# Chunked scan of a Mamba-2 layer on one core: mask, skip term and scaled x move to other engines, gate in one operation, products in another order

## The chip, the cores and the metric

The program runs on one core of a Trainium2 chip, in one launch. The metric is the time of that launch in microseconds, from runs on the chip. The core has a matrix engine (TensorE, PE in the profile), a vector engine (VectorE, DVE), an activation engine (ScalarE, ACT), a general engine (GpSimd, POOL) and a queue that issues transfers (SyncE, SP). The engines run side by side, each in the order in which its own instructions are written, and meet only at semaphores.

## The reference, cut to what matters

`x` is 2048 rows of 512. The program computes a Mamba-2 mixer and a feed-forward block, then a mixture of experts. The change touches the scan between the mixer's input projection and the feed-forward block:

```python
# per chunk of 128 rows (16 chunks), 16 heads of 64, in 4 groups of heads
dAc    = cumsum(dA)
Lm     = where(tril, exp(dAc[q] - dAc[s]), 0)             # decay, masked
Y_diag = einsum(C, B, Lm, x * dt)
states = einsum(B, exp(dAc[-1] - dAc), x * dt)
carry  = states + exp(dAc[-1]) * carry                    # from chunk to chunk
Y_off  = einsum(C, carry_before, exp(dAc))
y      = Y_diag + Y_off + D * x
y      = rmsnorm(y * silu(z), norm_w) @ out_proj_w
h      = residual + y
h2     = rmsnorm(h, ln2_w)                                # feeds the next stage
```

## The kernel before, in words

`project` (to about 272 us) computes x, B, C, z and dt and stores the rows `cv` (x, B and C of a chunk, channels on partitions) and `zs` (the gate, silu of z) to DRAM. `ssd`, the scan, goes over `TILES` = 16 tiles of 128 rows. `finish` is the feed-forward block and the experts. Data are float32, products of weights are split into three (`hi`/`lo` parts).

The order of each engine's work in `ssd` is written out by hand: one loop over c per engine, in which `e = c - 1` is the tile whose output is being finished and `f = c - 2` the one whose normed rows are turned for the next stage. In a tile PE does:

- `seg` (4 a tile): into one of two banks the mask, by a product of the identity with `mask_r` (L1152), and onto it the row sums of the decay (L1155). ACT's `exps` (L937) makes the decay from it, with the exponential;
- `b_dot_c` (2): B times C (L1164), by which DVE's `score` (L1026) multiplies the decay;
- `cum_rows` (2, L1179): ACT's `cum_exp` (L944) and DVE's `decayed_c` (L1049) make `cexp` of it;
- `diagonal` (2, L1192) and `carried` (2, L1204): 8 products each into the one bank `y_ps`, which DVE's `gate` reads: it adds `dx` (D·x, made by POOL's `skip_x`, L857) and, in a second operation, multiplies by `zs`;
- `states` (L1215), `rows` (L1225: the transposes of the next tile's `cv`, which ACT copies into `xb_row`, L963), `out_proj` (2 of 12 products, L1239), `row_sums` (L1247), `turn_h2` (L1255).

ACT's `high` (L950, L952) makes the upper part and the square of the gated y, DVE's `low` (L1032) the rest. DVE's `outcome` (L1064) makes `hres`; ACT's `h_squares` (L969) sums its squares; POOL's `second_norm` (L900 to L903) norms it, and POOL's `residual` (L894) adds it to x0. POOL also has `decayed_x` (L865), `decay_carry` (L874) and `row_scale` (L884 to L886). DVE's `scaled_x` (L1079) makes `xdt`, x times dt.

SP stores the sum that `residual` made and then loads `cv`, `zs` and `x0` for two tiles later:

```python
eng.wait_ge(s["xh"], e + 1)                      # e = c - 1: POOL's residual(e)
eng.dma_start(dr["xh"][e...], x0[e % 3]).then_inc(xh_st[e % 3], 16)
n = c + 2
ge(eng, xh_st[n % 3], 16 * (n // 3))             # that store has landed
eng.wait_ge(s["gate"], 2 * c + 2)                # and the buffers of tile c are read
load(n)                                          # cv, zs, x0
```

PE's `rows` waits for `cv` and `zs` together (both count on `cv_dma`).

Of the kernel before, what the change touches and what calls it, by code (L numbers as in the profile page):

```python
# [744 lines left out]
def ssd(nc, ins, dr, ident, ones, keep, ffT, first_weights, over):  # L745
# [6 lines left out]
    with ExitStack() as ctx:  # L752
        def sb(name, shape, dt=F32):
# [16 lines left out]
        dx = [sb(f"dx{i}", [P, HPG, P]) for i in range(2)]  # L770
# [18 lines left out]
            "seg", "exp", "cb", "score", "ebc", "ebx", "cexp", "yd", "yo", "ysum", "gate", "hi", "lo", "sq", "sqs", "rs",  # L789
# [57 lines left out]
        def _(eng):  # L847
# [4 lines left out]
            def skip_x(c, a):  # L852

                if a == 0:
                    eng.wait_ge(cv_dma[c % 2], 32 * (c // 2 + 1))
                ge(eng, s["ysum"], 2 * (c - 1) + a + 1)
                eng.tensor_tensor(dx[a][:, :, :], cv[c % 2][:, a, :].unsqueeze(1).broadcast_to([P, HPG, P]),  # L857
                                  d_col[:, a * HPG:(a + 1) * HPG].unsqueeze(2).broadcast_to([P, HPG, P]), ALU.mult)\
                   .then_inc(s["dx"], 1)
# [51 lines left out]
            eng.wait_ge(s["v_dma"], 16 * 9)  # L911
            for c in range(TILES + 1):
                e = c - 1
                if c < TILES:
                    for a in range(2):
                        skip_x(c, a)
                    if c + 1 < TILES:
                        decayed_x(c)
                        decay_carry(c)
                if e >= 0:  # L920
                    row_scale(e)
                    if c < TILES:
                        residual(e)
                    second_norm(e)
                    if c == TILES:
                        residual(e)

        @block.scalar
        def _(eng):
            def exps(c, hg):  # L930
# [8 lines left out]
                last.then_inc(s["exp"], 1)  # L939

# [37 lines left out]

            rows(0)
            for c in range(TILES + 2):  # L980
                e, f = c - 1, c - 2
                now, late, later = c < TILES, 0 <= e < TILES, 0 <= f
                if now:
                    exps(c, 0)
                    cum_exp(c, 0)
                    exps(c, 1)
# [4 lines left out]
                if now:  # L991
                    exps(c, 2)
                if c == 0:
                    out_high(HPG, NB)
# [4 lines left out]
                if now:  # L999
                    exps(c, 3)  # L1000
                    cum_exp(c, 1)
                    high(c, 0)
                    if c + 1 < TILES:
                        rows(c + 1)
                if late and now:
                    h_squares(e)

        @block.vector
        def _(eng):
            def gate(c, a):  # L1010

                eng.wait_ge(s["yo"], 2 * c + a + 1)
                eng.wait_ge(s["dx"], 2 * c + a + 1)
                ge(eng, s["lo"], 2 * (c - 1) + a + 1)
                ge(eng, s["sq"], 2 * (c - 1) + a + 1)
                if a == 0:
                    eng.wait_ge(cv_dma[c % 2], 32 * (c // 2 + 1))
                eng.tensor_tensor(yg[a][:, :, :], y_ps[:, :].rearrange("p (j q) -> p j q", j=HPG), dx[a][:, :, :], ALU.add)\
                   .then_inc(s["ysum"], 1)
                eng.wait_ge(s["ysum"], 2 * c + a + 1)  # L1020
                eng.tensor_tensor(yg[a][:, :, :], yg[a][:, :, :], zs[c % 2][:, a, :, :], ALU.mult).then_inc(s["gate"], 1)
# [52 lines left out]
            def scaled_x(c):  # L1074
                g, u = group(c)
                eng.wait_ge(s["xb_row"], c + 1)
                ge(eng, s["yd"], 2 * (c - 1))
                ge(eng, s["xdd"], c - 1)
                eng.tensor_tensor(xdt[c % 2][:, :].rearrange("p (g r d) -> p g r d", g=NG, r=HPG),  # L1079
                                  xb_row[c % 2][:, 0, :].rearrange("p (g d) -> p g d", g=NG).unsqueeze(2)  # L1080
                                  .broadcast_to([P, NG, HPG, HD]),
                                  dt_all[:, g, u * HEADS:(u + 1) * HEADS].rearrange("p (g r) -> p g r", g=NG).unsqueeze(3)
                                  .broadcast_to([P, NG, HPG, HD]), ALU.mult).then_inc(s["xdt"], 1)

# [20 lines left out]
            scaled_x(0)  # L1105
            for c in range(TILES + 2):
                e, f = c - 1, c - 2
                now, late, later = c < TILES, 0 <= e < TILES, 0 <= f
                if late:
                    gate(e, 1)  # L1110
                if now:
                    score(c, 0)
                    decayed_c(c, 0)
                    score(c, 1)
                if c == 0:
                    out_low(0, HPG)
                if late:
                    low(e, 1)
                    if now:
                        new_carry(e)  # L1120
                    squares(e)
                if now:
                    gate(c, 0)
                if late:
                    row_sums(e)
                if later and c != TILES:
                    h2_low(f)
                if now:
                    score(c, 2)
                    score(c, 3)  # L1130
                    if c == 0:
                        out_low(HPG, NB)
                    decayed_c(c, 1)
                    low(c, 0)
# [5 lines left out]
                if now:  # L1140
                    if c + 1 < TILES:
                        scaled_x(c + 1)
# [3 lines left out]
        def _(eng):  # L1146
            def seg(c, hg):

                g, u = group(c)
                ge(eng, s["exp"], 4 * c + hg - 1)  # L1150
                ps = seg_ps[hg % 2]
                eng.matmul(ps[:, :], ident_r[:, :], mask_r[:, :].unsqueeze(1).broadcast_to([P, HPG, P]),  # L1152
                           start=True, stop=False)
                m = u * NG + hg
                eng.matmul(ps[:, :], sel[:, m:m + 1].broadcast_to([P, P]), bd[:, g, :, :].rearrange("p j q -> p (j q)"),  # L1155
                           start=False, stop=True).then_inc(s["seg"], 1)
# [25 lines left out]
            def diagonal(c, a):  # L1182

                ge(eng, s["ysum"], 2 * c + a)
# [3 lines left out]
                for j in range(HPG):  # L1188
                    for b in range(2):
# [3 lines left out]
                                          decay[hg][:, j, :], start=(j == 0), stop=False, skip_group_check=True)  # L1193
# [64 lines left out]
            rows(0)  # L1258
            for c in range(TILES + 2):
# [963 lines left out]
```

## Time and profile before

| | |
|---|---|
| time, median of 3 runs (lowest to highest) | 1429.9 us (1429.3 to 1430.69) |
| the profiled execution's own time | 1429.85 us |
| its span in the profile | 1427.8 us |
| busy over the span: PE, DVE, ACT, POOL | 96%, 67%, 45%, 32% |
| the scan: first and last instruction of PE | 272.99 us to 563.5 us |
| from a tile's first `seg` to the next tile's | 17.33 us |

The span is what the profiler recorded of one execution; 2.05 us of its time lie around it. In a timeline a row is an instruction, or several in a row of one kind ("x4"), with its start and its length; the next one on the same engine can start before the length is over, because an engine overlaps the end of one with the start of the next, so what an instruction costs its engine in a busy stretch is the distance of two starts. In brackets stands how long the engine had been idle and what released it.

### The profile page before, as it was taken

The numbers are of one execution on the slowest core, as the hardware profiler recorded it, in microseconds if no ns is written. First come the engines' busy times: TensorE is split into PE (matmuls) and PEld (weight loads), VectorE is DVE, ScalarE is ACT, GpSimd is POOL, SyncE is SP. The second block draws the span as 40 slices with busy tenths as digits, with TensorE's granted clock in tenths as the row PEclk, the third lists the DMA queues.
The fourth block names the chain that finished last, engine by engine and source line by source line (L and its number), as shares of the span: only waits on it lengthen the run. The fifth ranks groups of instructions, "written<-read, shape, count | busy, mean of one in ns | idle before, by whom it ended". The sixth has DMA issues, their size and how long they took to land.

```text
span 1427.8 us, 20607 instructions
## 1 busy us (share of the span) xinstructions
PE 1374.9 (96%) x7240; PEld 1103.4 (77%) x7240; DVE 953.5 (67%) x1327; ACT 640.9 (45%) x1123; POOL 460.4 (32%) x447
## 2 busy tenths in 40 slices
PE   6899999899999997999999999999999889999998
PEld 5677778666666665888888888888887689999997
DVE  7789788789999996233333333333346879999997
ACT  5445445545555554221111212111212358888886
POOL 2112121357777775111010101110101026566563
PEclk9999999999999998999999999999999979999999
DMA  6133123722222232400000000002034924444331
GB/s 208 60 118 118 60 89 140 221 97 104 104 104 104 104 111 81 156 30 15 30 29 15 29 15 29 15 30 96 0 111 155 334 81 74 77 71 75 72 49 22
DMA packets 69047, 122.62 MB, mean 86 GB/s; under 512 B 11743, under 2 KB 28127, under 8 KB 68960
## 3 DMA queue, kind: packets, MB, share of 16 engines
q1 hardware_dynamic: 59696, 103.67, 21.3%
q0 software_dynamic: 8736, 16.79, 6.8%
q8 instruction: 49, 0.80, 0.2%
q10 hardware_dynamic: 528, 1.05, 0.2%
q14 instruction: 38, 0.31, 0.1%
HBM read 81.37 MB, written 43.78 MB: 88 GB/s over the span
## 4 chain that ended last, share of the span: by engine, by line
PE 57%; DVE 2%; ACT 0%; issue 0%; DMA 0%; POOL 0%; DVEq 0%; ACTq 0%; POOLq 0%
PE fin_bank L1934 54%; PE fin_bank L2075 1%; PE fin_bank L2094 1%; DVE onehot L1843 0%; PE fin_bank L2002 0%; DMA xs<-xn_rows,idx 0%; PE fin_bank L1990 0%; DVE ff_w_lo L1735 0%; ACT gu_hi L1626 0%; DVE fi_bn L1770 0%; ACT ff_w_hi L1604 0%; DVE gu_lo L1864 0%; PE fin_bank L2067 0%; POOL out_dram L1558 0%; PE fin_bank L2000 0%
## 5 line engine op out<-in xcount | busy, mean ns | idle before, releaser
L1697 DVE TENSOR_TENSOR ff_prod<-ff_prod,fin_bank 128x512 f32<-128x512 f32 x64 | 44.0, 688 | 263.0 <-PE fin_bank L1934 263.0
L1934 PE MATMUL fin_bank<-ff_hT_hi,ff_w_hi 128*128 128x512 f32 x512 | 202.8, 396 | 3.2 <-DVE ff_w_lo L1705 3.2
L1934 PE MATMUL fin_bank<-ff_hT_lo,ff_w_hi 128*128 128x512 f32 x512 | 202.7, 396 | 0.0
L1934 PE MATMUL fin_bank<-ff_hT_hi,ff_w_lo 128*128 128x512 f32 x512 | 202.6, 396 | 0.0
L1488 POOL TENSOR_TENSOR ff_w_lo<-ff_stage,ff_w_hi 128x1024 fp32r<-128x1024 f32 (+1 forms) x24 | 56.5, 2355 | 410.9 <-ACT ff_w_hi L1594 406.0
L1579 ACT ACTIVATE ff_prod<-fin_bank 128x512 f32<-128x512 f32 x64 | 38.3, 598 | 230.8 <-PE fin_bank L1934 230.7
L687 PE MATMUL pj_bank<-hT_hi,w_in_hi 128*128 128x512 f32 x324 | 131.5, 406 | 6.1 <-DVE w_in_lo L587 5.0
L555 DVE SCALAR_TENSOR_TENSOR conv_acc<-raw,conv_w,conv_acc 128x512 f32<-128x512 f32 x144 | 108.1, 751 | 37.2 <-ACT raw L355 32.1
L687 PE MATMUL pj_bank<-hT_lo,w_in_hi 128*128 128x512 f32 x324 | 128.6, 397 | 0.0
L687 PE MATMUL pj_bank<-hT_hi,w_in_lo 128*128 128x512 f32 x324 | 128.1, 395 | 0.0
L1864 DVE TENSOR_TENSOR gu_lo<-wx,gu_hi 128x1408 fp32r<-128x1408 f32 (+1 forms) x79 | 125.0, 1621 | 1.9 <-ACT gu_hi L1626 1.8
L1582 ACT ACTIVATE ff_p_hi<-ff_prod 128x512 fp32r<-128x512 f32 x64 | 40.5, 632 | 190.3 <-DVE ff_prod L1697 190.3
L1626 ACT ACTIVATE gu_hi<-wx 128x1408 fp32r (+1 forms) x79 | 109.8, 1391 | 19.4 <-DMA wx<-in_L_ffn_Wd_dram 15.6
L937 ACT ACTIVATE decay<-ss_bank,keep_neg_cum 128x128 f32<-128x128 f32 x256 | 73.0, 368 | 100.4 <-PE ss_bank L1155 100.4
L1934 PEld LDWEIGHTS fin_bank<-ff_hT_hi,ff_w_hi 128*128 128x128 f32 x512 | 96.4, 188 | 27.1 <-issue 3.6
L1755 DVE TENSOR_TENSOR acc_rows<-fin_bank,acc_rows 128x512 f32<-128x512 f32 x128 | 87.5, 689 | 40.7 <-PE fin_bank L1934 40.3
L1934 PEld LDWEIGHTS fin_bank<-ff_hT_hi,ff_w_lo 128*128 128x128 f32 x512 | 96.3, 188 | 23.7
L1934 PEld LDWEIGHTS fin_bank<-ff_hT_lo,ff_w_hi 128*128 128x128 f32 x512 | 96.3, 188 | 23.5
L1934 PE MATMUL fin_bank<-gu_hi,xe_hi 128*128 128x352 f32 x312 | 105.1, 337 | 0.0
L1934 PE MATMUL fin_bank<-gu_lo,xe_hi 128*128 128x352 f32 x312 | 101.0, 324 | 0.0
L1934 PE MATMUL fin_bank<-gu_hi,xe_lo 128*128 128x352 f32 x312 | 100.8, 323 | 0.0
L1934 PE MATMUL fin_bank<-ff_w_lo,ff_p_hi 128*128 128x512 f32 x256 | 100.1, 391 | 0.0
(299 smaller groups left out, 3171.4 us busy)
## 6 DMA issues: line engine op xcount, KB each, us to landing
cv_rows<-cst SPq DMA_DIRECT2D x12, 1024.0 KB, 4.2
cv<-cv_rows SPq DMA_DIRECT2D x16, 768.0 KB, 4.3
zs_rows<-zst SPq DMA_DIRECT2D x8, 1024.0 KB, 6.5
zs<-zs_rows SPq DMA_DIRECT2D x16, 512.0 KB, 5.3
wx<-in_L_ffn_Wg_dram SPq DMA_DIRECT2D x8, 704.0 KB, 8.9
wx<-in_L_ffn_Wu_dram SPq DMA_DIRECT2D x8, 704.0 KB, 9.4
x<-_attn_hidden_states_dram SPq DMA_DIRECT2D x16, 256.0 KB, 5.5
xh_rows<-x SPq DMA_DIRECT2D x16, 256.0 KB, 2.0
```

The lines of the kernel that those rows point to most:

```text
L555: eng.scalar_tensor_tensor(acc[m % 4][:, :], raw[m % 3][:, t:t + GR], conv_w[:, ch, t:t + 1], acc[m % 4][:, :], ALU.mult, ALU.add).then_in ...
L687: mm = eng.matmul(ps[:, :], (w_hi, w_lo)[a][:, k, col:col + P], x[b][:, k, :], start=(k == 0 and t == 0), stop=(k == KD - 1 and t == 2))
L937: last = eng.activation(decay[hg][:, j, :], seg_ps[hg % 2][:, j * P:(j + 1) * P], ACT.Exp, bias=neg_cum[:, g, h:h + 1])
L1488: eng.tensor_tensor(w_lo[par][j][:, cols], stage[j][:, cols], w_hi[par][j][:, cols].bitcast(F32), ALU.subtract).then_inc(s["w_lo"], 1)
L1579: eng.activation(prod[c][:, :], gate_ps[c][:, :], ACT.Silu).then_inc(s["silu"], 1)
L1582: eng.activation(p_hi[k % 2][:, c, :], prod[c][:, :], ACT.Copy).then_inc(s["p_hi"], 1)
L1626: eng.activation(out, raw_part(own[j], kind), ACT.Copy).then_inc(s["ew_hi"], 1)
L1697: eng.tensor_tensor(prod[c][:, :], prod[c][:, :], up_ps[c][:, :], ALU.mult).then_inc(s["prod"], 1)
L1755: eng.tensor_tensor(row, down_ps[t][:, :], row, ALU.add).then_inc(s["add"], 1)
L1864: eng.tensor_tensor(lo, raw_part(own[j], kind), hi.bitcast(F32), ALU.subtract).then_inc(s["ew_lo"], 1)
L1934: mm = eng.matmul(ps, w[a], x[b], start=first and i == 0, stop=last and i == 2)
L2075: last = eng.transpose(xT_ps[:, k * P:(k + 1) * P], xs[j % UN][:, k * P:(k + 1) * P], ident[:, :])
```

## The change

- PE's `seg` no longer writes the mask, but for the first two: ACT's new `mask` copies `mask_r` into the bank as soon as `exps` has read it, and PE's one product adds to it.
- `skip_x` moves from POOL to ACT. It writes D·x into `y_ps` (four operations of 128 columns), `diagonal` adds to it, and `gate` is one operation, `y_ps` times `zs`. `y_ps` is written again only after `gate` has read it.
- `scaled_x` moves from DVE to POOL, behind `row_scale`, and `residual` from ahead of `second_norm` to behind it.
- PE's products stand in another order, and `seg(c + 1, 0)` comes at the end of tile c. ACT's and DVE's order is changed too.

```diff
@@ POOL
-            def skip_x(c, a):
-                ...
-                ge(eng, s["ysum"], 2 * (c - 1) + a + 1)
-                eng.tensor_tensor(dx[a][:, :, :], cv[c % 2][:, a, :].unsqueeze(1)..., d_col[...]..., ALU.mult)
+            def scaled_x(c):
+                eng.wait_ge(s["xb_row"], c + 1)
+                ge(eng, s["yd"], 2 * (c - 1))
+                ge(eng, s["xdd"], c - 1)
+                eng.tensor_tensor(xdt[c % 2]..., xb_row[c % 2]..., dt_all..., ALU.mult).then_inc(s["xdt"], 1)
...
+            scaled_x(0)
             for c in range(TILES + 1):
                 e = c - 1
-                if c < TILES:
-                    for a in range(2):
-                        skip_x(c, a)
-                    if c + 1 < TILES:
-                        decayed_x(c)
-                        decay_carry(c)
+                if c + 1 < TILES:
+                    decayed_x(c)
+                    decay_carry(c)
                 if e >= 0:
                     row_scale(e)
-                    if c < TILES:
-                        residual(e)
+                if c + 1 < TILES:
+                    scaled_x(c + 1)
+                if e >= 0:
                     second_norm(e)
-                    if c == TILES:
-                        residual(e)
+                    residual(e)
@@ ACT
+            def mask(c, hg):
+                n = 4 * c + hg
+                if n < 4 * TILES - 2:
+                    eng.wait_ge(s["exp"], n + 1)
+                    eng.activation(seg_ps[hg % 2]..., mask_r..., ACT.Copy).then_inc(s["masked"], 1)
...
+            def skip_x(c, a):
+                ...
+                ge(eng, s["gate"], 2 * c + a)
+                for j in range(HPG):
+                    last = eng.activation(y_ps[:, j * P:(j + 1) * P], cv[c % 2][:, a, :], ACT.Copy,
+                                          scale=d_col[:, a * HPG + j:a * HPG + j + 1])
+                last.then_inc(s["dx"], 1)
@@ DVE
             def gate(c, a):
                 eng.wait_ge(s["yo"], 2 * c + a + 1)
-                eng.wait_ge(s["dx"], 2 * c + a + 1)
...
-                eng.tensor_tensor(yg[a]..., y_ps..., dx[a]..., ALU.add).then_inc(s["ysum"], 1)
-                eng.wait_ge(s["ysum"], 2 * c + a + 1)
-                eng.tensor_tensor(yg[a]..., yg[a]..., zs[c % 2]..., ALU.mult).then_inc(s["gate"], 1)
+                eng.tensor_tensor(yg[a]..., y_ps..., zs[c % 2]..., ALU.mult).then_inc(s["gate"], 1)
@@ PE
             def seg(c, hg):
-                ge(eng, s["exp"], 4 * c + hg - 1)
-                eng.matmul(ps[:, :], ident_r[:, :], mask_r..., start=True, stop=False)
+                ps, n = seg_ps[hg % 2], 4 * c + hg
+                if n < 2:
+                    eng.matmul(ps[:, :], ident_r[:, :], mask_r..., start=True, stop=False)
+                else:
+                    eng.wait_ge(s["masked"], n - 1)
...
             def diagonal(c, a):
-                ge(eng, s["ysum"], 2 * c + a)
+                eng.wait_ge(s["dx"], 2 * c + a + 1)
```

The order of the instructions on two engines follows; line numbers of the changed kernel are its own. First PE, in one tile in the middle, of the kernel before: from the transposes of the next tile (L1225) to the first product of `out_proj` (L1239).

```order
L1225 MATMUL ss_bank<-ident,cv 128x128 x4
L1192 MATMUL ss_bank<-decay,xdt 64x128 x8
L1204 MATMUL ss_bank<-cexp,carry 64x128 x8
L1215 MATMUL ss_bank<-xdd,xb_row 64x256 x4
L1152 MATMUL ss_bank<-keep_mask_r,keep_ident_r 128x512
L1155 MATMUL ss_bank<-keep_bd,keep_sel 128x512
L1179 MATMUL ss_bank<-keep_bd,sel_wide 128x512
L1164 MATMUL ss_bank<-cv 128x512 x2
L1152 MATMUL ss_bank<-keep_mask_r,keep_ident_r 128x512
L1155 MATMUL ss_bank<-keep_bd,keep_sel 128x512
L1239 MATMUL ss_bank<-wo_hi,y_hi 128x512
```

And PE of the changed kernel, of the same place, from the two products ahead of the transposes (now L1239; `out_proj` is L1253, `seg` L1169, `cum_rows` L1193, `b_dot_c` L1178).

```order
L1193 MATMUL ss_bank<-keep_bd,sel_wide 128x512
L1169 MATMUL ss_bank<-keep_bd,keep_sel 128x512
L1239 MATMUL ss_bank<-ident,cv 128x128 x4
L1206 MATMUL ss_bank<-decay,xdt 64x128 x8
L1218 MATMUL ss_bank<-cexp,carry 64x128 x8
L1229 MATMUL ss_bank<-xdd,xb_row 64x256 x4
L1178 MATMUL ss_bank<-cv 128x512 x2
L1193 MATMUL ss_bank<-keep_bd,sel_wide 128x512
L1169 MATMUL ss_bank<-keep_bd,keep_sel 128x512
L1253 MATMUL ss_bank<-wo_hi,y_hi 128x512
```

The mask's products are gone, and the products that use the whole array stand together: `cum_rows` is next to `seg`, and the first `seg` of the next tile has moved ahead of the transposes.

POOL, one tile, of the kernel before: `row_scale` (L884 to L886), `residual` (L894), `second_norm` (L900 to L903), `skip_x`, `decayed_x`, `decay_carry`.

```order
L884 TENSOR_SCALAR small<-small 128x1
L885 TENSOR_TENSOR small<-small,ss_half_neg 128x1
L886 TENSOR_SCALAR small<-small 128x1
L894 TENSOR_TENSOR x_1<-hres,x_1 128x512
L900 TENSOR_SCALAR small<-small 128x1
L901 TENSOR_TENSOR small<-small,ss_half_neg 128x1
L902 TENSOR_SCALAR h_1<-hres,small 128x512
L903 TENSOR_TENSOR h_1<-h_1,ln_row 128x512
L857 TENSOR_TENSOR dx<-cv,keep_d_col 128x512 x2
L865 TENSOR_TENSOR xdd<-xdt,keep_exp_suf 128x1024
L874 TENSOR_TENSOR carry<-carry,keep_chunk_decay 128x512
```

And POOL of the changed kernel, the same tile (`scaled_x` is L856, `second_norm` L901 to L904, `residual` L895).

```order
L885 TENSOR_SCALAR small<-small 128x1
L886 TENSOR_TENSOR small<-small,ss_half_neg 128x1
L887 TENSOR_SCALAR small<-small 128x1
L856 TENSOR_TENSOR xdt<-xb_row,keep_dt 128x1024
L901 TENSOR_SCALAR small<-small 128x1
L902 TENSOR_TENSOR small<-small,ss_half_neg 128x1
L903 TENSOR_SCALAR h_1<-hres,small 128x512
L904 TENSOR_TENSOR h_1<-h_1,ln_row 128x512
L895 TENSOR_TENSOR x_1<-hres,x_1 128x512
L866 TENSOR_TENSOR xdd<-xdt,keep_exp_suf 128x1024
L875 TENSOR_TENSOR carry<-carry,keep_chunk_decay 128x512
```

`residual` now stands behind the transposes' consumer `scaled_x` and behind the whole of `second_norm`. ACT, one tile of the changed kernel, from the second `cum_exp` (L952) to the next tile's first `skip_x` (L995); `mask` is L945, `exps` L936, `h_squares` L977, `high` L958 and L960.

```order
L952 ACTIVATE ebx<-ss_bank 128x512
L971 ACTIVATE xb_row<-ss_bank 128x512
L936 ACTIVATE decay<-ss_bank,keep_neg_cum 128x128 x4
L945 ACTIVATE ss_bank<-keep_mask_r 128x512
L977 ACTIVATE ss_junk,small<-hres 128x512
L952 ACTIVATE ebx<-ss_bank 128x512
L936 ACTIVATE decay<-ss_bank,keep_neg_cum 128x128 x4
L958 ACTIVATE y_hi<-yg 128x512
L960 ACTIVATE sq<-yg 128x512
L995 ACTIVATE ss_bank<-cv,keep_d_col 128x128 x4
```

Here `exps` of the next tile's first group and `mask` have come between the copy of the transposed rows (L971) and `h_squares` (L977), and `skip_x` stands behind `exps` and `high`.

## Rows read from the trace of the kernel before

**Rows 1.** Windows, one stretch: busy us (and instructions) of each engine, PEclk, DMA

```profile
400.00:450.00 50.00, 49.76 (x366) 33.92 (x366) 46.30 (x56) 26.62 (x74) 36.24 (x36) 1.00 0.30 110
```

**Rows 2.** Timeline, PE, one tile: start, length, what, count [idle before <-releaser]

```profile
396.61 0.50 PE L1152 MATMUL ss_bank<-keep_mask_r,keep_ident_r 128*128 128x512 f32 x1
396.95 0.40 PE L1155 MATMUL ss_bank<-keep_bd,keep_sel 128*128 128x512 f32 x1
397.18 0.39 PE L1179 MATMUL ss_bank<-keep_bd,sel_wide 128*128 128x512 f32 x1
...
399.13 0.39 PE L1239 MATMUL ss_bank<-wo_hi,y_hi 128*128 128x512 f32 x1
...
402.02 1.09 PE L1192 MATMUL ss_bank<-decay,xdt 128*64 128x128 f32 x16
...
410.35 0.60 PE L1225 MATMUL ss_bank<-ident,cv 128*128 128x128 f32 x4
...
413.94 0.50 PE L1152 MATMUL ss_bank<-keep_mask_r,keep_ident_r 128*128 128x512 f32 x1
```

**Rows 3.** Timeline, ACT, the later half of the same tile

```profile
407.52 1.14 ACT L937 ACTIVATE decay<-ss_bank,keep_neg_cum 128x128 f32<-128x128 f32 x4 [1.13 <-PE ss_bank L1155]
408.53 0.61 ACT L944 ACTIVATE ebx<-ss_bank 128x512 f32<-128x512 f32 x1
409.01 0.66 ACT L950 ACTIVATE y_hi<-yg 128x512 fp32r<-128x512 f32 x1
409.53 0.66 ACT L952 ACTIVATE sq<-yg 128x512 f32<-128x512 f32 x1
410.98 0.60 ACT L963 ACTIVATE xb_row<-ss_bank 128x512 f32<-128x512 f32 x1 [0.80 <-PE ss_bank L1225]
411.48 0.62 ACT L969 ACTIVATE ss_junk<-hres 128x512 bf16<-128x512 f32 x1
412.00 0.19 ACT L969 ACTIVATION_READ_ACCUMULATOR ss_junk<-hres 128x1 f32 x1
```

**Rows 4.** Timeline, POOL, the next tile

```profile
411.38 1.26 POOL L894 TENSOR_TENSOR x<-hres,x 128x512 f32<-128x512 f32 x1 [3.39 <-DVE hres L1064]
412.73 1.05 POOL L900 TENSOR_SCALAR small<-small 128x1 f32<-128x1 f32 x1
...
414.72 1.58 POOL L902 TENSOR_SCALAR h<-hres,small 128x512 f32<-128x512 f32 x1
416.39 1.29 POOL L903 TENSOR_TENSOR h<-h,ln_row 128x512 f32<-128x512 f32 x1
417.63 2.93 POOL L857 TENSOR_TENSOR dx<-cv,keep_d_col 128x512 f32<-128x512 f32 x2
420.53 1.90 POOL L865 TENSOR_TENSOR xdd<-xdt,keep_exp_suf 128x1024 f32<-128x1024 f32 x1
```

**Rows 5.** Timeline, POOL, after the last tile

```profile
551.24 0.25 POOL L900 TENSOR_SCALAR small<-small 128x1 f32<-128x1 f32 x1
```

**Rows 6.** Timeline, DVE, beside rows 4

```profile
411.61 2.12 DVE L1079 TENSOR_TENSOR xdt<-xb_row,keep_dt 128x1024 f32<-128x1024 f32 x1 [0.31 <-ACT xb_row L963]
...
416.66 1.56 DVE L1049 TENSOR_TENSOR cexp<-cv,ebx 128x512 f32<-128x512 f32 x1
```

**Rows 7.** Timeline, SP's queue: start and length of each issue

```profile
412.68 0.32 SPq L825 DMA_DIRECT2D xh_rows<-x  x1
416.01 0.32 SPq L812 DMA_DIRECT2D cv<-cv_rows  x1
```

**Rows 8.** DMA issues of 300 to 545 us: count, KB each, us to landing

```profile
zs<-zs_rows SPq DMA_DIRECT2D x13, 512.0 KB, 5.3
xh_rows<-x SPq DMA_DIRECT2D x14, 256.0 KB, 2.0
```

**Rows 9.** Timeline, ACT, the first tile

```profile
277.38 2.57 ACT L976 ACTIVATE wo_hi<-wo_raw,keep_normw 128x512 fp32r<-128x512 f32 x4
```

**Rows 10.** Timeline, PE, the first tile

```profile
278.37 1.09 PE L1192 MATMUL ss_bank<-decay,xdt 128*64 128x128 f32 x16 [2.04 <-DVE decay L1026]
```

More of the change, by code:

```diff
@@ L977, in out_high @@
                        .then_inc(s["wo_hi"], 1)
+            def skip_x(c, a):
+                if a == 0:
+                    eng.wait_ge(cv_dma[c % 2], 32 * (c // 2 + 1))
+                if c + a == 0:
+                    eng.wait_ge(s["seg"], 1)
+                ge(eng, s["gate"], 2 * c + a)
[3 more added lines that the diff above has]
+                last.then_inc(s["dx"], 1)
             rows(0)
+            eng.wait_ge(s["v_dma"], 16 * 9)
+            exps(0, 0)
+            mask(0, 0)
             for c in range(TILES + 2):
@@ L991, in _ @@
                 if now:
+                    skip_x(c, 0)
+                    mask(c, 1)
                     exps(c, 2)
+                    mask(c, 2)
                 if c == 0:
@@ L1000, in _ @@
                     exps(c, 3)
+                    high(c, 0)
+                    skip_x(c, 1)
+                    mask(c, 3)
                     cum_exp(c, 1)
-                    high(c, 0)
                     if c + 1 < TILES:
                         rows(c + 1)
+                        exps(c + 1, 0)
+                        mask(c + 1, 0)
                 if late and now:
@@ L1072, in last_norm @@
                    .then_inc(s["h2_step"], 2)
[L1074 to L1083, printed above, removed]
             def new_carry(c):
@@ L1110, in _ @@
                     gate(e, 1)
+                    if now:
+                        new_carry(e)
                 if now:
+                    decayed_c(c, 0)
                     score(c, 0)
-                    decayed_c(c, 0)
                     score(c, 1)
@@ L1258, in _ @@
             rows(0)
+            eng.matmul(y_ps[:, :], ident_r[:, :], mask_r[:, :].unsqueeze(1).broadcast_to([P, HPG, P]), start=True, stop=True)
+            seg(0, 0)
             for c in range(TILES + 2):
@@ L1269, in _ @@
                 if now:
+                    seg(c, 2)
                     diagonal(c, 0)
-                    seg(c, 2)
                     carried(c, 0)
-                if late and now:
-                    row_sums(e)
                 if later and c != TILES:
@@ L1278, in _ @@
                     b_dot_c(c, 1)
+                if late and now:
+                    row_sums(e)
+                if now:
                     seg(c, 3)
-                    cum_rows(c, 1)
                 if late:
                     out_proj(e, 1, None if now else row_sums)
+                if now:
+                    cum_rows(c, 1)
+                    if c + 1 < TILES:
+                        seg(c + 1, 0)
                 if c == TILES:
```

46 lines of the change are left out of this document (20 added, 26 removed).

## The prediction, made before the changed kernel ran

> **What bounds the kernel now.** I began with the windows. In the middle of the scan PE is busy for 49.76 of 50 us at the full granted clock, DVE for 46.30, POOL for 36.24, ACT for 26.62 [rows 1]. Then the timeline of PE over one tile: from one tile's first `seg` to the next tile's lie 17.33 us (396.61 to 413.94), and no row between them carries a wait [rows 2]. So in the tiles of the middle PE is the bound. ACT waits often, but only for PE (1.13 us before `exps`, 0.80 us before the copy into `xb_row`) [rows 3]. POOL's row for `residual` shows 3.39 us of idle time [rows 4]. SP issues the store of `residual`'s sum at 412.68 and `cv` at 416.01 [rows 7]; that `cv` serves transposes that PE makes at about 427.7, one period of 17.33 behind those at 410.35 [rows 2]. With `zs` issued some 0.35 later and landing in 5.3 us [rows 8], the data are there at about 421.7: 6 us to spare. That reserve is what I follow below, because the change spends it.
>
> **What PE saves.** A mask product holds PE for 0.34 us (396.61 to 396.95), the one behind it for 0.23 (396.95 to 397.18) [rows 2]. I read the extra 0.11 as the price of going from products on part of the array to whole ones: it comes with the first whole product, not with the mask. On the way back there is about 0.1 as well: 12 products of `out_proj` take 2.89 us up to the `diagonal` behind them (399.13 to 402.02), 0.13 more than 12 times 0.23 [rows 2]. Removed per tile: 4 x 0.23 = 0.92. The new order goes from part to whole three times a tile and not five: 2 x (0.11 + 0.1) = 0.4. Together 1.3, so PE's own work falls from 17.33 to 16.0 us a tile.
>
> **What the others gain and lose.** ACT now has 26.62 / 50 x 17.33 = 9.2 us a tile. It gets four `mask` of 128x512 and eight operations of 128x128 for D·x. No row shows ACT writing a bank; the nearest are copies of 128x512 at a distance of 0.50 to 0.52 us and 0.60 to 0.66 long, and four of 128x128 at 1.01 us together and 1.14 long [rows 3]. I bound a `mask` between 0.45 and 0.65 and take 0.50; `skip_x` between 0.8 and 1.15, taking 1.0. ACT comes to 9.2 + 4 x 0.50 + 2 x 1.0 = 13.2 us, not a bound by load. The Trainium skill, "PSUM — Partial Sum Buffer", specifications, says that ScalarE's write is faster into PSUM than into SBUF; no row here shows it, and by it both would stand at the lower end, 0.05 us a `mask` less. DVE loses `scaled_x` (2.12 us [rows 6]) and two additions and is no bound. POOL loses two `dx` (2.93 us) and gets `scaled_x`: as many elements as `decayed_x` in 1.90 us or as both `dx` in 2.93 [rows 4]. I take 1.9 to 2.3, near `decayed_x`, which also reads one full tensor and one spread along 64.
>
> **New waits of PE.** `y_ps` must hold D·x before `diagonal`. For the first half ACT can start only when the product of `cum_rows` is through, about 0.5 us after its start: then `cum_exp` 0.49 (408.53 to 409.01), `exps` 1.01, `high` 2 x 0.52, `skip_x` 1.14 with its length [rows 3], and the handovers, 0.5 + 0.49 + 1.01 + 1.04 + 1.14 + 0.1 = 4.3 us. PE itself needs 0.34 + 0.23 + 2.89 + 0.23 = 3.7 from there to `diagonal`. That is a stall of 0.55 a tile (0.3 to 0.8). For the second half ACT has, from `seg(c, 3)` on, `exps`, `high`, `skip_x`, `mask`, `cum_exp`, and then DVE `decayed_c`: 0.4 + 1.01 + 1.04 + 1.0 + 0.5 + 0.62 + 0.7 + 0.1 = 5.4 us, against 0.24 + 2.8 + 0.5 + 0.6 + 1.0 = 5.2 on PE to `carried`: 0.2 more (0 to 0.6). Behind the waiting `skip_x` on ACT stand `mask` and the next `exps`, which PE needs only later. PE with its stalls: 16.0 + 0.55 + 0.2 = 16.7 us.
>
> **The loop that spends the reserve.** SP loads tile c + 2 only when the store of `residual(c - 1)` has landed. Before, `residual` ran as soon as `hres` was there. Now it stands behind `scaled_x(c + 1)`, which waits for the transposes `rows(c + 1)`, and behind `second_norm`. And `rows(c + 2)`, one tile on, waits for that load. This closes a loop of one tile:
>
> - landing of `zs` to the transposes and their copy's start on ACT: 0.05 + 0.63 (410.35 to 410.98) [rows 2, 3] = 0.68;
> - ACT: copy 0.50, `exps` with its full length 1.14 (`mask` waits for it), `mask` 0.50, `h_squares` 0.52 + 0.19 [rows 3], handovers 0.15: 3.0. POOL's `scaled_x` lies beside it: 0.60 + 1.9 = 2.5;
> - `second_norm`: 4.95 from 412.73 to 417.68, less 0.80, because its first step took 1.05 there while DVE ran `xdt`, and 0.25 alone [rows 4, 5, 6]: 4.15;
> - `residual` 1.26 [rows 4] and 0.05: 1.31;
> - the store 2.0 [rows 8] and two handovers: 2.1;
> - `cv` issued, `zs` 0.35 later and 5.3 to its landing [rows 7, 8]: 5.65, with handover 5.7.
>
> The sum is 16.9 us. Without handovers and with a `mask` of 0.45 it is 16.5. To it comes what POOL loses to DVE: DVE's `cexp` of the next tile falls, by this count, into `second_norm`'s two long steps. Rows 4 and 6 show such meetings: the first step stretched from 0.25 to 1.05 beside `xdt`, `cexp` to 1.56 beside L903. I add 0.2 and take 17.1. That is above PE's 16.7, so PE would wait for DMA at the transposes, some 0.4 us a tile, and nearly all of the 1.3 us is given back.
>
> **The sum.** The loop counts between `rows(2)` and `rows(15)`, 13 periods: 13 x (17.1 - 17.33) = -3.0 us. At the edges: in the first tile four copies of `out_proj`'s weights, 2.57 us [rows 9], stand ahead of the first `skip_x` on ACT, so the first `diagonal` (278.37, where PE had already waited 2.04 us [rows 10]) comes some 2.8 us later. I estimate that 1.6 of it are left when tile 1 starts, and that tile 1, which PE still bounds, gives 0.9 back: +0.7. The last tile has no transposes behind it and saves 1.3 less the stalls: -0.6; the one-operation `gate` in the tail, -0.3. Edges -0.2, all -3.2. From the profiled execution's own 1429.85 (span 1427.8 and 2.05 around it), 0.05 under the median of 1429.9, that is 1426.7 us. The stages behind the scan don't change.
>
> **The rivals.**
>
> PE stays the bound. If `mask`, the norm or the landing are some tenths shorter, the loop is under 16.7 and PE's stalls decide: 13 x (16.7 - 17.33) - 0.2 = -8.4, 1421.5 us. With no stall either, 16.0: -17.5, 1412.4. For it speaks that the loop's lower bound is 16.5 and that PE is now busy without a gap; against it that this needs six terms at their short end, and ACT two chains as well.
>
> The loop is longer than before's period, slower. The place is POOL, from `scaled_x` to the end of `residual`; the price is one lost turn against DVE for each meeting. If `cexp` gets in ahead of the norm's last step, and DVE's `low` of the other half ahead of `residual`, each costs up to DVE's 0.6 to 0.7: 16.9 + 0.6 + 0.6 = 18.1, or 17.7 with one whole and a third of the other. It decides from 17.35 on. At 17.7: 13 x 0.37 - 0.2 = +4.6, 1434.4 us; at 18.1: +9.8, 1439.6. `scaled_x` at 2.93 instead of 1.9 would make POOL later than ACT by 0.5 and adds as much. For it speaks that in rows 4 and 6 nearly every operation of POOL meets one of DVE's; against it that `xdt`, DVE's longest operation with two tensors in SBUF, is gone from DVE. The Trainium skill, "SBUF — State Buffer", on engine ports, has the shared port pair of VectorE and GpSimd as an exclusive lock for a whole instruction, so that the later one blocks fully. By that rule the first step's 1.05 is waiting, and rows 4 and 6 agree (`xdt` ends at 413.73, the step at 413.78). By it a `cexp` that gets in costs `second_norm` about 0.65 each tile, the loop is 17.6 and the time about 1433.
>
> The change doesn't do what it says. `skip_x` could be so late that `diagonal` waits for it 1.3 us and more: then PE alone has 17.3 and nothing is won, 1430. It would need ACT operations of twice the rows' length.
>
> **How the numbers follow.** Loop between 16.9 and 17.55: 0.5, time 1424 to 1432.5; below 17.12, which half of this case is, the gain is over 0.2%. PE bound: 0.25, all faster. Loop over 17.55: 0.22, all slower. No effect by late `skip_x`: 0.03. About 0.2%, 2.9 us, is what a measurement of this kernel can tell from no change. Faster 0.25 + 0.25 = 0.50, within 0.28, slower 0.22. The range leaves out the stall-free end at 1412.4 and the meetings that all go against POOL: 1414 to 1438. The likeliest case's own range is 1424 to 1432.5.
>
> **What would show it.** Right: in the changed kernel's PE timeline a wait of some tenths to 1 us before each set of transposes, released by the DMA into `zs` or `cv`; `cv` issued some 2 us after the store, and the store issued a third of a tile into the next tile, not at its end; a period of 17 us; a wait of about 0.5 us before the first `diagonal` of each tile; mask products gone, `mask` near 0.5. Wrong: transposes without a wait and a period under 16.8 (the loop is shorter than I count), a period of 17.5 and more with `second_norm` over 4.7 (the meetings), or PE idle before `seg` (a `mask` that comes too late). A scan that is no different but a time that is would mean that I looked at the wrong stage.

## The result, and the profile after

| | before | changed |
|---|---|---|
| time, median (lowest to highest) of 6 runs each | 1429.38 us (1428.86 to 1430.69) | 1437.28 us (1434.46 to 1438.6) |
| span of the profiled execution | 1427.8 us | 1435.9 us |
| busy over the span: PE, DVE, ACT, POOL | 96%, 67%, 45%, 32% | 95%, 62%, 49%, 31% |

The changed kernel takes 1.0049 times as long (95% interval 1.0039 to 1.0059). Slightly faster was forecast, 1426.7 us. The measured time lies just inside the stated range (1414 to 1438), but at its slow end, which only the second rival reached, and the direction is the wrong one. The window in the middle of the scan [rows 1], of the changed kernel, with the same columns:

```profile
400.00:450.00 50.00, 46.51 (x334) 31.46 (x330) 33.83 (x46) 39.58 (x109) 32.89 (x33) 1.00 0.31 111
```

PE now has gaps, 3.5 us of 50, at the full clock. The waits of the scan's middle (300 to 548 us) of the changed kernel, us in total, times, longest, tell for whom:

```profile
POOL xdt L856 <- ACT xb_row L971: 58.8, 14, 6.3
PE ss_bank L1206 <- ACT ss_bank L995: 8.9, 14, 0.6
PE ss_bank L1239 <- DMA zs<-zs_rows: 8.4, 12, 2.4
```

The waits of the kernel before show none of PE for DMA there; now it waits 12 times at the transposes (L1239), for `zs`, and 14 times, 0.6 us each, for ACT's `skip_x` (L995) at the first `diagonal` of a tile. The second stall that was forecast, before `carried`, shows only twice here.

One turn of the loop, row by row. PE's timeline of the changed kernel [rows 2]:

```profile
414.80 0.65 PE L1239 MATMUL ss_bank<-ident,cv 128*128 128x128 f32 x4 [0.43 <-DMA zs<-zs_rows]
...
423.90 1.09 PE L1206 MATMUL ss_bank<-decay,xdt 128*64 128x128 f32 x16 [0.64 <-ACT ss_bank L995]
...
432.26 0.66 PE L1239 MATMUL ss_bank<-ident,cv 128*128 128x128 f32 x4 [0.70 <-DMA zs<-zs_rows]
```

ACT's [rows 3]:

```profile
413.20 1.26 ACT L995 ACTIVATE ss_bank<-cv,keep_d_col 128x128 f32<-128x128 f32 x4
414.38 0.60 ACT L945 ACTIVATE ss_bank<-keep_mask_r 128x512 f32<-128x512 f32 x1
414.89 0.60 ACT L952 ACTIVATE ebx<-ss_bank 128x512 f32<-128x512 f32 x1
415.49 0.60 ACT L971 ACTIVATE xb_row<-ss_bank 128x512 f32<-128x512 f32 x1
415.99 1.14 ACT L936 ACTIVATE decay<-ss_bank,keep_neg_cum 128x128 f32<-128x128 f32 x4
417.16 0.60 ACT L945 ACTIVATE ss_bank<-keep_mask_r 128x512 f32<-128x512 f32 x1
417.69 0.61 ACT L977 ACTIVATE ss_junk<-hres 128x512 bf16<-128x512 f32 x1
```

POOL's [rows 4]:

```profile
416.17 1.90 POOL L856 TENSOR_TENSOR xdt<-xb_row,keep_dt 128x1024 f32<-128x1024 f32 x1 [3.95 <-ACT xb_row L971]
418.49 0.19 POOL L901 TENSOR_SCALAR small<-small 128x1 f32<-128x1 f32 x1 [0.41 <-ACT ss_junk L977]
...
421.09 1.45 POOL L904 TENSOR_TENSOR h<-h,ln_row 128x512 f32<-128x512 f32 x1
422.51 1.79 POOL L895 TENSOR_TENSOR x<-hres,x 128x512 f32<-128x512 f32 x1
```

DVE's, beside it [rows 6]:

```profile
422.48 0.69 DVE L1058 TENSOR_TENSOR y_lo<-yg,y_hi 128x512 fp32r<-128x512 f32 x1
```

And SP's queue [rows 7]:

```profile
424.33 0.32 SPq L824 DMA_DIRECT2D xh_rows<-x  x1
426.46 0.32 SPq L811 DMA_DIRECT2D cv<-cv_rows  x1
426.82 0.43 SPq L812 DMA_DIRECT2D zs<-zs_rows  x1
```

Each step starts where the one before it ends, read from these rows: transposes 414.80, copy 415.49, norm 418.49, `residual` 422.51, store 424.33, `cv` 426.46, next transposes 432.26. The period is 17.46 us where it was 17.33.

Where the 8.1 us of the two spans come from, by the starts of the transposes (`rows(n)`), with `finish` from its first product:

| stretch | before | changed | difference | forecast |
|---|---|---|---|---|
| `rows(0)`, the scan's start | 272.99 | 274.04 | +1.05 | 0 |
| `rows(0)` to `rows(2)` | 33.44 | 36.43 | +3.0 | +0.7 |
| `rows(2)` to `rows(15)`, 13 periods | 225.11 | 228.6 | +3.5 | -3.0 |
| `rows(15)` to `finish` | 35.21 | 35.16 | -0.05 | -0.9 |
| the rest of the program | | | +0.6 | 0 |

The first and the last line are outside the change. In the traces of all the kernels here `rows(0)` lies between 272.34 and 274.06 us, with the same code ahead of it, so +1.05 is the spread of single executions; +0.6 is of the same size.

Eleven of the 13 periods have a mean of 17.38. The other two are 19.19 and 18.24, each with a late landing in it. In the first it is a store's. The DMA issues of the changed kernel from 510 to 518 us: count, KB, us to landing [rows 8]:

```profile
xh_rows<-x SPq DMA_DIRECT2D x1, 256.0 KB, 3.9
```

In SP's queue `cv` stands behind it:

```profile
511.17 0.32 SPq L824 DMA_DIRECT2D xh_rows<-x  x1
515.07 0.32 SPq L811 DMA_DIRECT2D cv<-cv_rows  x1
```

The other stores of the scan landed in 2.0 to 2.2 us. PE waited 2.42 us, and in the next window its granted clock was 0.83, a mean of the two levels (1.2 and 2.4 GHz), where 400 to 450 us had 1.00. In the second period the `zs` issued at 532.87 landed in 6.2 us, 0.9 more than the usual 5.3. The window:

```profile
520.00:530.00 10.00, 9.17 (x60) 6.52 (x61) 4.58 (x8) 5.24 (x15) 6.78 (x6) 0.83 0.07 26
```

### The profile page after: what moved, and what is told of

The parts are those of the page before. It is cut to its first block, busy times and chain, and to the rows that moved or that the text cites. A ratio compares the mean times of both kernels' runs of the same rounds, so it can differ in the third digit from the quotient of the medians.

```text
span 1435.9 us, 20597 instructions
## 1 busy us (share of the span) xinstructions
PE 1361.5 (95%) x7179; PEld 1095.8 (76%) x7179; DVE 889.7 (62%) x1279; ACT 710.3 (49%) x1313; POOL 438.3 (31%) x431
## 3 DMA queue, kind: packets, MB, share of 16 engines
q10 hardware_dynamic: 528, 1.05, 0.2%
## 4 chain that ended last, share of the span: by engine, by line
PE 56%; DVE 2%; issue 1%; DMA 0%; ACT 0%; POOL 0%; DVEq 0%; POOLq 0%; ACTq 0%
PE fin_bank L1953 53%; PE fin_bank L2094 1%; PE fin_bank L2113 1%; DVE onehot L1862 0%; DMA xs<-xn_rows,idx 0%; PE fin_bank L2021 0%; PE fin_bank L2009 0%; DVE ff_w_lo L1754 0%; DMA out_dram<-result_rows,idx 0%; DVE fi_bn L1789 0%; ACT ff_w_hi L1623 0%; PE fin_bank L2086 0%; POOL out_dram L1577 0%; DVE oj L1857 0%; PE fin_bank L2019 0%
## 5 line engine op out<-in xcount | busy, mean ns | idle before, releaser
L1953 PE MATMUL fin_bank<-ff_w_hi,ff_p_hi 128*128 128x512 f32 x256 | 99.9, 390 | 0.0
```

The costliest lines, as they stand in the source:

```text
L1953: mm = eng.matmul(ps, w[a], x[b], start=first and i == 0, stop=last and i == 2)
```

## Experiments

Every ratio is to the kernel before, on the same chip, with its 95% interval. Three chips were used, on which the kernel before took 1429.66 (the runs a), 1430.36 (b1, b2, b4, c1) and 1429.89 us (b3, d1); where two runs of different groups differ by less than that, nothing is read from it. The theory: the loop through POOL, the store and the load of `cv` and `zs` sets the period. The rivals: PE's stalls behind ACT, or DVE.

**Open the loop, two ways.** a1_residual_ahead:

```diff
                 if e >= 0:
-                    second_norm(e)
                     residual(e)
+                    second_norm(e)
```

> The changed kernel with one edit: POOL does residual(e) ahead of second_norm(e), still behind scaled_x. Theory (a loop of one tile: transposes, scaled_x, second_norm, residual, store, load, transposes): the store goes out some 4 us earlier, the waits for DMA before the transposes are gone, the tile is PE's own 16.7 to 16.8 us (17.46 less the wait of 0.70), 13 x (16.76 - 17.58) = -10.7 us against the changed kernel, about 1427. Rival (the DMA wait only covers another one: h2 comes late for turn_h2, or ACT's chains stretch to the same length): 1433 or more.

a2_load_before_store, SP:

```diff
+                    load_rows(n)                 # cv, zs: waits only for tile c's readers
                 if e >= 0:
                     eng.wait_ge(s["xh"], e + 1)
                     eng.dma_start(dr["xh"]..., x0[e % 3]...)
-                    load(n)                      # cv, zs, x0
+                    load_x(n)                    # x0 alone
```

> The changed kernel with one edit in SP's order: cv and zs of tile c + 2 are loaded when tile c's buffers are read, ahead of the wait for residual(c - 1) and its store; only x0 is loaded behind the store. POOL's order stays. Theory of the loop: cut at its other end, same effect, about 1427, with cv issued at the start of a tile. Rival (the transfers themselves are slower beside the new order of work, or residual is late for another reader): no change from the changed kernel, 1437.

1430.71 us, ratio 1.0004 (0.9995 to 1.0013), and 1431.09 us, 1.0008 (0.9999 to 1.0017). In both PE has no wait for DMA, and the period is 17.12 to 17.17 in each tile. One edit is on POOL, the other on SP, and what they share is that the load no longer waits for the norm: the loop is the cause of the wait for DMA. Both times are 4 us over the expected 1427, because a stall that the changed kernel hardly shows has come out (below). In POOL's and SP's timelines of a1_residual_ahead the store is now at 417.60:

```profile
416.13 1.45 POOL L895 TENSOR_TENSOR x<-hres,x 128x512 f32<-128x512 f32 x1
```

```profile
417.60 0.32 SPq L824 DMA_DIRECT2D xh_rows<-x  x1
419.62 0.32 SPq L811 DMA_DIRECT2D cv<-cv_rows  x1
```

With the loop open a late landing costs nothing: the `zs` issued at 488.59 landed in 7.1 us, and the periods around it stayed at 17.15 and 17.14. What is left of PE's idle in a tile stands in its timeline:

```profile
414.55 1.09 PE L1218 MATMUL ss_bank<-cexp,carry 64*64 64x128 f32 x16 [0.53 <-DVE cexp L1075]
422.03 1.09 PE L1206 MATMUL ss_bank<-decay,xdt 128*64 128x128 f32 x16 [0.63 <-ACT ss_bank L995]
```

Counted from start to start, less what the product ahead takes, that is 0.60 and 0.68; PE's own work is 17.15 - 1.28 = 15.87.

**Lengthen the loop.** a3_longer_loop: POOL makes one more product of `decay_carry`'s shape (1.04 us), which nobody reads, between `second_norm` and `residual`.

```diff
                     second_norm(e)
+                    extra_work(e)
                     residual(e)
```

> The changed kernel with one operation more on POOL between second_norm and residual, of the shape of decay_carry (1.04 us), whose result nobody reads. POOL is idle some 5 us a tile. Theory of the loop: every period gets about 1.0 to 1.1 us longer, 13 x 1.05 = +14, about 1451. Rival (POOL has idle time, the wait for DMA is a matter of transfer time): no change, 1437.

1446.3 us, ratio 1.0115 (1.0099 to 1.013): 9.0 over the changed kernel. `rows(2)` to `rows(15)` take 237.09, 0.65 a period more than in the changed kernel (228.6) for 1.04 put in; expected were 1451 us and 1.05. PE's waits are where the theory has them:

```profile
PE ss_bank L1246 <- DMA zs<-zs_rows: 18.7, 13, 1.8
```

Without the changed kernel's two late landings the mean of its other eleven periods is 17.38, and this kernel's mean is 18.24: 0.86 more. Its rows tell where the rest is. First POOL, then DVE and SP:

```profile
410.04 1.57 POOL L882 TENSOR_TENSOR extra<-ln_row,keep_chunk_decay 128x512 f32<-128x512 f32 x1
411.58 1.27 POOL L901 TENSOR_TENSOR x<-hres,x 128x512 f32<-128x512 f32 x1
```

```profile
410.03 0.69 DVE L1065 TENSOR_TENSOR y_lo<-yg,y_hi 128x512 fp32r<-128x512 f32 x1
```

```profile
412.88 0.32 SPq L825 DMA_DIRECT2D xh_rows<-x  x1
```

The new operation takes 1.57 us beside `y_lo`, and `residual`, now behind it, is back at 1.27 where the changed kernel has 1.79. So the store goes out 10.57 us behind the transposes in the mean of the 13 tiles, where the eleven tiles of the changed kernel have 9.59: 0.98 of the 1.04 has come through. Then `zs` happened to land in 5.21 us here and in 5.34 there, 0.13 less. That is the 0.86.

**The stalls alone, and both.** b1_skip_early: each `skip_x` goes ahead of what it stood behind on ACT, of `cum_exp`, `exps` and `high` in the first half of the tile and of `exps` and `high` in the second. b2_both: b1 with `residual` ahead of the norm.

```diff
+                    skip_x(c, 0)
                     cum_exp(c, 0)
                     exps(c, 1)
                 ...
                     high(e, 1)
-                    skip_x(c, 0)
                     mask(c, 1)
...
+                    skip_x(c, 1)
                     exps(c, 3)
                     high(c, 0)
-                    skip_x(c, 1)
                     mask(c, 3)
```

> The changed kernel with one edit in ACT's order: skip_x(c, 0) ahead of cum_exp(c, 0), skip_x(c, 1) ahead of exps(c, 3), where ACT sits idle for 1.7 and 1.1 us. POOL's order stays, so the loop over residual, store and load stays. Theory (the loop sets the period, PE's stalls for D*x lie in its shadow): the waits before diagonal and carried (0.68 and up to 0.6 us) go, the wait for DMA before the transposes grows by as much, the time stays within 2 us of the changed kernel's 1437. Rival (PE's own stalls set the period and the DMA wait follows them): 13 x 1.2 = -16, 1421.

> Both edits: residual ahead of second_norm on POOL, and skip_x where ACT is idle. With residual ahead alone the tile was 17.15 us, of which 0.68 before the first diagonal and 0.60 before the second carried were waits, so PE's own work is 15.87. Theory: both waits go, 13 x (15.9 - 17.15) = -16 and some 1 to 2 us in the first and last tile, about 1413. Rival (the next limit is close, DVE's lock with POOL or ACT's queue): 1418 to 1424.

b1: 1436.18 us, 1.0037 (1.0023 to 1.0051). The wait at `diagonal` is gone, and the time is that of the changed kernel within the two intervals; the idle has moved to the transposes (8.4 us in the changed kernel):

```profile
PE ss_bank L1239 <- DMA zs<-zs_rows: 17.5, 12, 2.2
```

b2: 1413.49 us, 0.9883 (0.9868 to 0.9898), as expected, period 15.84 to 15.85. Its window:

```profile
400.00:450.00 50.00, 50.00 (x384) 34.71 (x380) 39.59 (x51) 43.27 (x118) 36.06 (x35) 1.00 0.35 129
```

With the loop open, the stalls are worth 17.2 us (1430.71 to 1413.49); with it closed, about 1, which these runs cannot tell from nothing. The two waits hide each other.

**The first tile.** b3_first_tile (the changed kernel) and b4_all (b2) put ACT's copies of `out_proj`'s weights behind the masks of the first tile, and DVE's part of the last four at that tile's end. The cut shows the first four; the last four go behind `mask(1, 0)`:

```diff
-                if c == 0:
-                    out_high(0, HPG)
                 ...
                     mask(c, 1)
+                if c == 0:
+                    out_high(0, HPG)
```

> The changed kernel with one edit, in the first tile alone: ACT's copies of out_proj's weights stand behind the masks instead of ahead of the first skip_x, and DVE's share of them at the end of that tile. Theory (the first tile's late skip_x is a cost of its own, separate from the loop): the first diagonal comes about 2.5 us earlier, rows(2) 1 to 2 us earlier, the 13 periods behind it as in the changed kernel (about 228 us): 1 to 2 us less than the changed kernel, 1435.5. Rival (the loop absorbs it: the store and the load set rows(2) too, so what the first tile gains is waited for at rows(2) or rows(3)): rows(3) at the same time as in the changed kernel, time the same within 0.5 us.

> As the one with both edits, and in the first tile ACT makes the copies of out_proj's weights later: the first four behind mask(0, 1), the last four behind mask(1, 0), DVE's lower parts of the last four at the tile's end. Theory: the first tile's diagonals no longer wait for 2.5 us of copies, PE's clock does not fall there, another -2 to -4 us, about 1410. Rival (the copies are only waited for later, by out_proj of tile 0): no gain, 1413.

b3: 1434.78 us, 1.0029 (1.002 to 1.0038), 2.5 under the changed kernel, where 1 to 2 were expected. From `rows(0)` to `rows(3)` it takes 51.53, where the changed kernel takes 53.94: the first tile is a cost of its own. (2.5 is about the spread of the changed kernel's own runs; the trace, not the median, carries this.) b4: 1412.33 us, 0.9876 (0.9861 to 0.9891), the fastest of all; 1.2 gained where 2 to 4 were expected. `rows(0)` to `rows(2)` falls from 38.07 in b2 to 36.33 only, and a new wait for `score` has come up. DVE's second four copies now run from 292.17 for 4.39 us, with `gate` behind them at 296.48; that they cause the wait is likely, but the steps between were not followed. Its PE, first tiles:

```profile
301.07 1.98 PE L1207 MATMUL ss_bank<-decay,xdt 128*64 128x128 f32 x16 [4.01 <-DVE decay L1053]
```

**Parts alone, on the kernel before.** a4_mask_alone gives only the mask to ACT:

```diff
-                eng.matmul(ps..., ident_r..., mask_r..., start=True, stop=False)
+                if n < 2:
+                    eng.matmul(ps..., ident_r..., mask_r..., start=True, stop=False)
+                else:
+                    eng.wait_ge(s["wide"], n)    # ACT's mask
```

> The kernel before with only the mask moved: ACT copies the mask into the banks (62 copies of 0.52 us), PE keeps one product for each seg; order, skip term, gate and scaled_x as before. Theory 1 (0.23 us of a mask product are its own, 0.11 are the switch to whole products): 62 x 0.23 = -14.3, about 1415. Theory 2 (all 0.34 are the mask's): -21, about 1408. Rival (DVE, 46.3 of 50 us busy, becomes the bound at 16.1 to 16.5 us a tile with its waits): -8 to -12, 1418 to 1421.

1426.05 us, 0.9973 (0.9962 to 0.9984), period 17.06: a smaller gain than either theory or the rival expected (1408 to 1421). PE's timeline of it:

```profile
397.60 0.50 PE L1172 MATMUL ss_bank<-keep_bd,keep_sel 128*128 128x512 f32 x1
397.93 0.39 PE L1256 MATMUL ss_bank<-wo_hi,y_hi 128*128 128x512 f32 x1
398.16 0.39 PE L1256 MATMUL ss_bank<-wo_lo,y_hi 128*128 128x512 f32 x1
...
404.12 0.38 PE L1264 MATMUL ss_bank<-ones,sqs 128*128 128x2 f32 x2 [0.66 <-DVE sqs L1054]
```

The `seg` product now has the distance 0.33 that the mask's had [rows 2], and the ones behind it 0.23. PE's own work is 17.06 - 0.67 = 16.39, 0.94 less: four times 0.23. What PE does not get is the 0.67, a wait for DVE at `row_sums`, where DVE's timeline has no wait between 395.60 and 407.19.

c1_mask_scaled: that kernel with `scaled_x` on POOL, behind `residual` and ahead of the norm.

> The kernel before with the mask moved to ACT and scaled_x moved to POOL, behind residual and ahead of second_norm; skip term, two-operation gate and PE's order as before. With the mask alone the tile was 17.06 us, of which PE waited 0.67 for DVE's sum of squares. Theory (DVE is the bound there, and 2.12 us of it are scaled_x): PE's own 16.4 a tile, 14 x -0.67 = -9, about 1417. Rival (POOL, with both dx and scaled_x 14.5 us and its locks against DVE, becomes late): 1424 or more.

1426.71 us, 0.9975 (0.9965 to 0.9986), where 1417 was expected: no gain over a4 in all. The middle gains a little, the period is 16.94 (1.7 us over the 13); the first tiles lose it again, `rows(0)` to `rows(2)` takes 36.34 where a4 has 33.41. There PE waits for a `cexp` that stands behind DVE's copies of the weights:

```profile
293.49 1.97 PE L1222 MATMUL ss_bank<-cexp,carry 64*64 64x128 f32 x16 [4.68 <-DVE cexp L1079]
```

PE's wait at `row_sums` stayed as it was although DVE's busy time in the window fell from 47.32 to 44.70:

```profile
PE ss_bank L1265 <- DVE sqs L1069: 8.9, 14, 0.7
```

So DVE's load does not set it. Neither expectation had this. In c1's trace the square that `sqs` sums is ready at 403.44, and `sqs` starts at 404.83: ahead of it on DVE stand `score`, which waits 0.40 us for an `exps` of ACT, then `y_lo` and the new carry. That this chain is the cause was not tried.

d1_before_residual_behind: only `residual` moves, behind the norm.

```diff
                     row_scale(e)
+                    second_norm(e)
                     if c < TILES:
                         residual(e)
-                    second_norm(e)
```

> The kernel before, with POOL's residual moved behind second_norm and nothing else. Theory (a loop, closed only because scaled_x stands on POOL ahead of the norm): here the norm starts with hres, at the place where residual was, so residual ends about 5 us later and the store lies at about 417.7 instead of 412.7. cv was issued 1.3 us behind the store's landing before, for another wait, so its issue moves by some 3.8 us only, to about 419.8, and zs lands at about 425.5, 2 us ahead of the transposes (427.7). No wait of PE at the transposes, period 17.33, time within 0.1% of before. Rival (residual's place alone is what costs): a wait of PE for DMA at the transposes in each tile and a period of 17.5 and more, +3 us and more.

1433.42 us, 1.0022 (1.0013 to 1.0031): I expected nothing, and it costs 3.5 us. Counted from the transposes, the store goes out after 8.19 us and not after 2.33 [rows 2, 7]: 5.9 later and not 5. The norm now waits for ACT's `h_squares`, which `residual` used to cover, 0.9, and `residual` itself takes 1.78. POOL's timeline:

```profile
412.54 0.62 POOL L900 TENSOR_SCALAR small<-small 128x1 f32<-128x1 f32 x1 [3.86 <-ACT ss_junk L969]
...
417.00 1.78 POOL L894 TENSOR_TENSOR x<-hres,x 128x512 f32<-128x512 f32 x1
```

In most tiles the 1.5 us left suffice (period 17.34). Two stores landed late, in 3.9 and 4.3 us, and SP's queue shows what the second does:

```profile
365.56 0.32 SPq L825 DMA_DIRECT2D xh_rows<-x  x1
369.90 0.32 SPq L812 DMA_DIRECT2D cv<-cv_rows  x1
```

4.34 us from store to `cv`. The transposes waited, and the two periods were 17.70 and 18.23; the next, 17.74, has a wait of 0.42 for DVE's `sqs` and a `zs` that landed in 7.4 us. In the profiled execution `rows(2)` to `rows(15)` is 1.9 us longer than before. It was the fastest of the eleven; that the others had more of it I did not see.

This displaced tile also shows what stretches `residual`. Here it starts 0.30 ahead of DVE's `cexp`, and `cexp` is the long one:

```profile
381.97 1.30 POOL L894 TENSOR_TENSOR x<-hres,x 128x512 f32<-128x512 f32 x1
```

```profile
382.27 1.54 DVE L1049 TENSOR_TENSOR cexp<-cv,ebx 128x512 f32<-128x512 f32 x1
```

In the tile shown above `cexp` starts 0.07 ahead of `residual` (417.00), and `residual` is the long one, 1.78:

```profile
416.93 0.68 DVE L1049 TENSOR_TENSOR cexp<-cv,ebx 128x512 f32<-128x512 f32 x1
```

In the same kernel, the one that comes second is stretched.

## Why the prediction was wrong

The loop was right; three sizes were too small, and together they turned a small gain into a loss. The time came out on the far side of the point that the second rival named: "It decides from 17.35 on". Of the forecast's -3.2 us, 3.6 were lost to the longer loop, 2.7 to two late landings, 2.3 in the first tile and 0.9 in the last; that makes +6.3, and the rest of the 8.1 is the first and the last line of the table. A loop of 17.38 alone would have given no change (13 x 0.05 - 0.2), not a loss.

- **The loop: 17.1 forecast, 17.46 in the tile shown, 17.38 in the mean of the undisturbed ones.** Term by term, forecast and measured: transposes to copy 0.68, 0.69; copy to norm 3.0, 3.00; `second_norm` 4.15, 4.02; `residual` 1.31, 1.82; store 2.1, 2.13; load 5.7, 5.80. The step that failed is the term for `residual` and its meeting with DVE. I had put the meetings at 0.2 in all, and on `cexp` in the norm. The meeting came from `y_lo`, with `residual` itself, in twelve tiles, in which it takes 1.79 to 1.82 us: `y_lo` ran from 422.48 to 423.17 and `residual` took 1.79 instead of 1.26 [rows 4], 0.53 more for the 0.66 that `y_lo` still ran. The sum `sqs` does not do it: in a3 `residual` runs beside it and takes 1.27. The Trainium skill, "SBUF — State Buffer", on engine ports, says of a VectorE instruction with two inputs in SBUF, as `y_lo` has, and a GpSimd instruction that reads SBUF that the one that starts later is blocked until the other is over. These rows agree, with 0.53 for 0.66. I had it as the cause of a rival, with 0.65 and on the norm, and should have laid DVE's new order beside POOL's to see which operation falls there. The norm was 0.13 shorter than forecast, so the mean is 17.38 and not more: 13 x (17.38 - 17.1) = 3.6 us.
- **The late landings.** "the store 2.0" and 5.3 for `zs` were medians. In this chain each landing counts: a store of 3.9 us cost 19.19 - 17.38 = 1.8, and a `zs` of 6.2 us most of 18.24 - 17.38 = 0.9. The kernel before had a `zs` of 6.4 us (issued at 381.73) and lost nothing by it. That the changed kernel's six runs spread over 4 us and the before's over 2 fits this, but only one execution was profiled.
- **The first tile: +0.7 forecast, +3.0 measured.** The delay itself was sized well: the first `diagonal` came 3.0 us later after `rows(0)` (8.37, before 5.38), where I had said 2.8. What failed is the rest, that only 1.6 of it would be left when tile 1 starts and that tile 1 would give 0.9 back: `rows(1)` comes 3.3 later (13.71, before 10.44), and tile 1 gives back 0.3 (22.72, before 23.01). PE, first tiles [rows 10]:

```profile
282.41 1.98 PE L1206 MATMUL ss_bank<-decay,xdt 128*64 128x128 f32 x16 [4.62 <-ACT ss_bank L995]
290.84 1.09 PE L1206 MATMUL ss_bank<-decay,xdt 128*64 128x128 f32 x16 [2.49 <-ACT ss_bank L995]
293.34 1.97 PE L1218 MATMUL ss_bank<-cexp,carry 64*64 64x128 f32 x16 [1.41 <-DVE cexp L1075]
```

  The 1.98 and 1.97, for what takes 1.09 at the full clock, show that the clock had fallen behind the waits; the granted clock from 282.40 to 284.30 us is 0.50, the lower level. The kernel before has such a row too, but one and not two:

```profile
288.89 1.97 PE L1204 MATMUL ss_bank<-cexp,carry 64*64 64x128 f32 x16 [2.16 <-DVE cexp L1049]
```

  b3, which moves the copies, brings `rows(0)` to `rows(2)` from 36.43 to 33.96, near the 33.44 of before.
- **The last tile: -0.9 forecast, -0.05 measured.** Only with both waits gone does it come: `rows(15)` to `finish` takes 33.64 in b2, and 34.96 and 34.88 in a1 and b1. What holds it in those two I did not follow.
- **PE's saving was right**: own work 15.87, forecast 16.0; a mask product 0.23; the switch 0.11. So were ACT's prices: `mask` 0.52 apart, forecast 0.50; `skip_x` 1.17, forecast 1.0 and just over its bound of 1.15; `scaled_x` 1.90.
- **PE's stalls were 0.68 and, once the loop is open, 0.60; forecast 0.55 and 0.2.** They cost next to nothing here, since the loop was longer. But with them PE would have had 17.15, not 16.7: the first rival ("PE stays the bound", 1421.5) could not have come at that price. a1 and a2, in which it did, took 1431.
- **The reserve.** The forecast found the right thing to follow: a load that had 6 us to spare had none. d1 adds that the place of `residual` alone spends 4.5 of the 6.

Shown by the runs: the loop (a1, a2, and a3 with its size), the stalls behind it (b1, b2), the first tile (b3), the mask's 0.23 (a4). Shown by rows, with no run of its own: that a meeting with DVE makes `residual`'s 0.53 (a3, d1). Open: how often landings are late in executions that were not profiled, and what holds PE at `row_sums` in a4 and c1.

## What to carry to other kernels

Before moving a consumer behind other work, find what its end releases, and go round once: if a buffer's store, the next load and the operation that waits for the load close a ring, add it up with each engine's new neighbours, and give it a margin for late landings, since a ring pays for each of them. When two waits cover each other, neither removal shows its worth by itself: here 7 us and 1, and 24 for both. The gain of the change (1.2%) was there, behind two small edits of order.

## What the runs showed of the hardware

- A 256 KB store landed in 2.0 to 2.1 us in most tiles; in 3.9 once in the changed kernel, in 3.9 and 4.3 in d1; never over 2.3 in a3 and b2. A 512 KB `zs` landed mostly in 5.0 to 5.6, in single cases in 6.2 (the changed kernel), 7.1 (a1) and 7.4 (d1).
- The first whole-array product behind products on part of the array costs 0.10 to 0.11 us more (0.34, then 0.23), whichever product it is: the mask's before, `seg`'s in a4.
- ACT writing 128x512 into a bank (`mask`): 0.60 long and 0.51 to 0.53 to the next start in the changed kernel, where its copy out of a bank (`xb_row`) has 0.60 and 0.50.
- POOL and DVE, both with operands in SBUF: `residual`'s 1.26 became 1.79 beside one DVE operation of 0.69 that had started just ahead of it; 0.30 ahead of `cexp` (d1) it kept its 1.30, and `cexp` took 1.54 in place of 0.68.
